# Inverse roots placed one tick later and built from fewer instructions, and the second layer's values copied out of PSUM by VectorE

## The reference, cut to what matters

```python
qkv = h @ wqkv;  q, k, v = jnp.split(qkv, 3, axis=-1)
q = l2norm(q) * qs;  k = l2norm(k) * ksc        # 1 / root of the sum of squares per head
q, k = rotary_xpos(q, k)
o = local_attention(q, k, v)                    # QK_SCALE = 8, window 64, softmax
x = x + o @ wo
h = (h - mu) / jnp.sqrt(var + 1e-05) * lg + lb  # layer norm, then a gated GELU
```

## Time and profile before

| what | us |
|---|---|
| median of 3 runs | 2072.57 (2064.77 to 2075.15) |
| the profiled execution | 2064.33 |
| its span, first to last instruction | 2062.5 |
| TensorE busy | 1760.4 |
| VectorE busy | 1278.5 |
| ScalarE busy | 1186.3 |
| GpSimd busy | 863.4 |

### The profile page before, as it was taken

One profiled execution on the slowest core, in us unless ns is written; L12 is line 12 of the kernel. 1 busy time (PEld: TensorE's weight loads), 2 busy tenths in 40 slices (PEclk: granted clock), 3 DMA queues, 4 the chain that ended last, 5 costly groups with the idle time before them and its releaser, 6 DMA issues.

```text
span 2062.5 us, 38065 instructions
## 1 busy us (share of the span) xinstructions
PE 1760.4 (85%) x12532; PEld 1140.4 (55%) x12532; DVE 1278.5 (62%) x4211; ACT 1186.3 (58%) x3527; POOL 863.4 (42%) x993
## 2 busy tenths in 40 slices
PE   6679988998989888998899888988899797785776
PEld 4358764654566545664566456654566455463454
DVE  4434456566575667566766666666856666857764
ACT  2434547566666666656666675666666565453633
POOL 2633215643445233542544343433453355534640
PEclk9889999999999999999999999999999998897968
DMA  8146510000000000000000000000000000000000
GB/s 235 50 143 224 187 31 1 11 1 1 6 2 17 1 6 1 1 17 1 6 2 17 1 6 2 17 1 5 2 1 11 1 7 1 1 7 0 1 1 11
DMA packets 49724, 53.48 MB, mean 26 GB/s; under 512 B 6386, under 2 KB 42236, under 8 KB 49532
## 3 DMA queue, kind: packets, MB, share of 16 engines
q0 software_dynamic: 7808, 27.79, 4.1%
q1 hardware_dynamic: 41724, 23.26, 3.9%
HBM read 41.60 MB, written 9.44 MB: 25 GB/s over the span
## 4 chain that ended last, share of the span: by engine, by line
PE 47%; DVE 20%; ACT 7%; issue 6%; POOL 1%; DVEq 0%; ACTq 0%; POOLq 0%
PE ps L596 5%; PE ps L658 5%; PE ps L733 3%; PE ps L616 3%; PE ps L575 3%; PE ps L555 3%; DVE p L1042 3%; DVE big L1232 3%; PE ps L640 2%; PE ps L565 2%; DVE ss L1228 2%; PE ps L784 2%; PE ps L630 2%; PE ps L775 2%; PE ps L777 2%
## 5 line engine op out<-in xcount | busy, mean ns | idle before, releaser
L1342 POOL COPY rdx<-rden 128x256 f32<-128x256 f32 x256 | 100.2, 420 | 656.1 <-DVE rden L1059 651.9
L1042 DVE CUSTOM_DVE_ANT_0 p<-ps,mask 128x128 f32<-128x128 f32 (+1 forms) x512 | 152.3, 354 | 209.6 <-PE ps L588 201.8
L1042 DVE CUSTOM_DVE_ANT_0 p<-ps,mask,nrq 128x128 f32<-128x128 f32 x512 | 148.8, 347 | 181.8 <-PE ps L584 181.7
L596 PE MATMUL ps<-ident,p 128*128 128x128 f32 x1280 | 220.9, 297 | 29.2 <-ACT p L873 26.6
L873 ACT ACTIVATE p<-p,nmax 128x128 f32<-128x128 f32 (+1 forms) x512 | 226.3, 442 | 0.0
L872 ACT ACTIVATE p<-p,nmax 128x128 f32<-128x128 f32 x512 | 200.1, 391 | 37.9 <-DVE nmax L1042 37.2
L887 ACT ACTIVATE pt<-ps 128x384 f32<-128x384 f32 (+1 forms) x256 | 111.9, 437 | 190.6 <-PE ps L596 188.6
L733 PE MATMUL ps<-wqkv,hT 128*128 128x512 f32 x384 | 195.2, 617 | 28.5 <-ACT big L952 28.0
L596 PEld LDWEIGHTS ps<-ident,p 128*128 128x128 f32 x1280 | 143.5, 147 | 107.5 <-issue 90.9
L575 PE MATMUL ps<-k,q 64*128 64x128 f32 x1024 | 133.2, 338 | 37.8 <-DVE nmax L1042 17.2
L575 PEld LDWEIGHTS ps<-k,q 64*128 64x128 f32 x1024 | 82.5, 196 | 141.7 <-issue 83.6
(11 more groups left out here) (255 smaller groups left out, 4112.8 us busy)
## 6 DMA issues: line engine op xcount, KB each, us to landing
slots_in<-xn SPq DMA_DIRECT2D x1, 2560.0 KB, 14.3
v<-slots_in SPq DMA_DIRECT2D x20, 128.0 KB, 4.7
slots_out<-v SPq DMA_DIRECT2D x20, 128.0 KB, 1.8
big<-in_x SPq DMA_DIRECT2D x4, 512.0 KB, 6.0
x<-in_x SPq DMA_DIRECT2D x8, 256.0 KB, 3.7
out_x<-x SPq DMA_DIRECT2D x8, 256.0 KB, 2.3
wqkv<-in_wqkv SPq DMA_DIRECT2D x2, 768.0 KB
xn<-in_x SPq DMA_DIRECT2D x6, 256.0 KB, 3.3
```

Of the source, the lines that this page charges most:

```text
L596: last = nc.tensor.transpose(bank[:, j * P:(j + 1) * P], c.p[:, u % 4, j * P:(j + 1) * P], c.ident[:, :])
L1042: last = V.tensor_tensor_reduce(out=c.p[:, u % 4, a:b], in0=bank[:, a:b], in1=mask, scale=scale, scalar=3e38, op0=ALU.add, op1=ALU.min, ac ...
```

## The change

1. `newton_rsqrt` drops the shift (the halving of the bits is one multiplication) and does one cheap step and one longer one in place of three: 9 instructions for 11. The last is returned, not linked, so that the caller can hang its own semaphore on it.
2. `rr` writes the negative root straight to `c.rr`, which now has two halves by turn; `nrq` and the instruction that filled it (L1244) are gone. The factor of 8 went into the rotation table and the mask's constant. `rr` is 10 instructions for 13, `inverse_root` 10 for 12.
3. `rr` of layer 0 moves one tick later for 0 < b < 7, into the tick of `kn` and ahead of it.
4. In layer 1 ScalarE no longer copies v. VectorE does, in a stage `v1` of its own in the tick of that tile's `qkv`, behind the `mix` and `rot` of the tile before. It announces the copy on `v1_done`; TensorE's ring `mm` waits on that semaphore where the bank it wants held such a v. There are 32 such copies of 128x512.

```diff
@@ Plan.qkv_stages
-        self.put(at + TILES, "rr", b, l)
+        for t in range(TILES * l):
+            self.put(at + t, "v1", b, t)
+        self.put(at + TILES + (l == 0 and 0 < b < LAST), "rr", b, l)
         self.put(at + TILES + 1, "kn", b, l)
@@
-def newton_rsqrt(nc, link, r, v, scratch):
+def newton_rsqrt(nc, link, r, v, scratch, t, sign=1):
-    link(nc.vector.tensor_scalar(scratch.bitcast(INT32), v.bitcast(INT32), 1, None, ALU.logical_shift_right))
-    link(nc.vector.tensor_scalar(r.bitcast(INT32), scratch.bitcast(INT32), -1.0, RSQRT_MAGIC, ALU.mult, ALU.add))
-    for _ in range(3):
-        link(nc.vector.scalar_tensor_tensor(out=scratch, in0=r, scalar=-0.5, in1=r, op0=ALU.mult, op1=ALU.mult))
-        link(nc.vector.tensor_tensor(scratch, scratch, v, ALU.mult))
-        link(nc.vector.scalar_tensor_tensor(out=r, in0=scratch, scalar=1.5, in1=r, op0=ALU.add, op1=ALU.mult))
+    a, b, c3 = (sign * x for x in RSQRT_LAST)
+    link(nc.vector.tensor_scalar(r.bitcast(INT32), v.bitcast(INT32), -0.5, RSQRT_MAGIC, ALU.mult, ALU.add))
+    link(nc.vector.tensor_tensor(scratch, r, r, ALU.mult))
+    link(nc.vector.tensor_tensor(scratch, scratch, v, ALU.mult))
+    link(nc.vector.scalar_tensor_tensor(out=r, in0=scratch, scalar=RSQRT_FIRST, in1=r, op0=ALU.add, op1=ALU.mult))
+    link(nc.vector.tensor_tensor(scratch, r, r, ALU.mult))
+    link(nc.vector.tensor_tensor(scratch, scratch, v, ALU.mult))
+    link(nc.vector.tensor_scalar(t, scratch, c3, b, ALU.mult, ALU.add))
+    link(nc.vector.tensor_tensor(t, t, scratch, ALU.mult))
+    return nc.vector.scalar_tensor_tensor(out=r, in0=t, scalar=a, in1=r, op0=ALU.add, op1=ALU.mult)
@@ tensor: mm_bank
-        if mm.free(*name):
-            pe.wait_ge(c.mm_done, mm.free(*name))
+        lane, n = mm.before(*name)
+        if n:
+            pe.wait_ge((c.mm_done, c.v1_done)[lane], n)
@@ scalar: qkv
-        evacuate(c.v1[:, g % 2, t, :], "qkv", b, l, t, 2)
+        if l == 0:
+            evacuate(c.v1[:, g % 2, t, :], "qkv", b, l, t, 2)
@@ vector
+    def v1(b, t):
+        dve.wait_ge(c.mm_full, mm.full("qkv", b, 1, t, 2))
+        V.tensor_copy(c.v1[:, plan.turn[(b, 1)] % 2, t, :], c.mm_ps[mm.slot("qkv", b, 1, t, 2)][:, :]).then_inc(c.v1_done, 1)
+
@@ vector: rr
-        newton_rsqrt(nc, link, c.rr[:, :], c.ss[:, :], c.scratch[:, 0, :])
-        TS(c.nrq[:, g % 2, :, :], c.rr[:, :].rearrange("p (t a h) -> p t a h", t=TILES, a=2)[:, :, 0, :], -8.0, None, ALU.mult)\
+        newton_rsqrt(nc, link, c.rr[:, g % 2, :], c.ss[:, :], c.scratch[:, 0, :], c.scratch[:, 1, :], -1)\
             .then_inc(c.r_ready, 1)
```

More of the change, by code:

```diff
@@ L43 @@
 LAST = BLOCKS - 1
-RSQRT_MAGIC = 1597463007.0
+RSQRT_MAGIC = 1595932665.0
+RSQRT_FIRST = -2.38924456
+RSQRT_LAST = (-1.3199104070663452, 0.4360533356666565, -0.06482572108507156)
 class Common:
@@ L311, in inverse_root @@
     link(nc.vector.tensor_scalar(c.scratch[:, 0, 0:TILES], c.mv[:, :, 1], 1e-5, None, ALU.add))
-    newton_rsqrt(nc, link, c.rstd[:, :], c.scratch[:, 0, 0:TILES], c.scratch[:, 1, 0:TILES])
+    few = c.scratch[:, 1, :]
+    link(newton_rsqrt(nc, link, c.rstd[:, :], c.scratch[:, 0, 0:TILES], few[:, 0:TILES], few[:, TILES:2 * TILES]))
 def whiten(eng, out, x, mv, rstd, t):
@@ L405, in buffers @@
     c.ss = sb("ss", [P, TILES * 2 * HEADS1])
-    c.rr = sb("rr", [P, TILES * 2 * HEADS1])
-    c.nrq = sb("nrq", [P, LAYERS, TILES, HEADS1])
+    c.rr = sb("rr", [P, 2, TILES * 2 * HEADS1])
     c.stats = sb("stats", [P, TILES, 6])
@@ L438, in buffers @@
     c.high_done, c.highs = sem("high_done"), 0
+    c.v1_done = sem("v1_done")
     c.chain, c.pool_chain = sem("chain"), sem("pool_chain")
@@ L490, in count_units @@
                 for j in range(n):
-                    rings[ring].add((*seg, j))
+                    rings[ring].add((*seg, j), lane=int(seg[0] == "qkv" and seg[2] == 1 and j == 2))
             plan.combs[seg] = combs
@@ L603, in values @@
             if st.i == 0:
-                pe.wait_ge(c.mm_done, mm.done("qkv", st.b, st.part, END, 2) if st.kind else mm.done("v", st.b, st.part, END, 0))
+                if st.kind and st.part:
+                    pe.wait_ge(c.v1_done, mm.done("qkv", st.b, 1, END, 2))
+                else:
+                    pe.wait_ge(c.mm_done, mm.done("qkv", st.b, 0, END, 2) if st.kind else mm.done("v", st.b, st.part, END, 0))
         v = c.v1[:, plan.turn[(st.b, st.part)] % 2, :, :] if st.kind else c.v0[:, st.part, :, :]
@@ L1040, in masked @@
                 g = 2 * st.s + i
-                scale = c.nrq[:, turn % 2, g, 2 * st.i + h:2 * st.i + h + 1] if st.kind else -0.125
+                at = g * 2 * HEADS1 + 2 * st.i + h
+                scale = c.rr[:, turn % 2, at:at + 1] if st.kind else -0.125
                 last = V.tensor_tensor_reduce(out=c.p[:, u % 4, a:b], in0=bank[:, a:b], in1=mask,
@@ L1251, in kn @@
         for t in range(TILES):
-            k_over_norm(V, c, t).then_inc(c.kn_ready, 1)
+            k_over_norm(V, c, g % 2, t).then_inc(c.kn_ready, 1)
     def glu(b, l):
@@ L1277, in vector @@
              "ln1n": ln1n, "ln2": ln2, "ln2n": ln2n, "phi": phi, "sum": total, "o1": o1, "s1": s1, "mix": mix, "rot": rot,
-             "rr": rr, "kn": kn, "glu": glu, "down1": down1, "fin": fin}
+             "rr": rr, "kn": kn, "v1": v1, "glu": glu, "down1": down1, "fin": fin}
     for i in range(4):
@@ L1287, in vector @@
     link(last)
-    var, tmp = c.few[:, 0:ALL], c.few[:, ALL:2 * ALL]
+    var, tmp, more = (c.few[:, i * ALL:(i + 1) * ALL] for i in range(3))
     link(TS(var, c.mv_all[:, :, 1], 1e-5, None, ALU.add))
-    newton_rsqrt(nc, link, c.rstd_all[:, :], var, tmp)
+    link(newton_rsqrt(nc, link, c.rstd_all[:, :], var, tmp, more))
     dve.sem_inc(c.stats_ready, 1)
@@ L1322, in vector, with k_over_norm @@
                 stage[seg[0]](*seg[1:])
-def k_over_norm(eng, c, t):
+def k_over_norm(eng, c, turn, t):
     kk = c.qkr[:, t, INNER1:2 * INNER1].rearrange("p (h d) -> p h d", h=HEADS1)
     at = (t * 2 + 1) * HEADS1
-    return eng.tensor_tensor(kk, kk, c.rr[:, at:at + HEADS1].unsqueeze(2).to_broadcast([P, HEADS1, HD]), ALU.mult)
+    return eng.tensor_tensor(kk, kk, c.rr[:, turn, at:at + HEADS1].unsqueeze(2).to_broadcast([P, HEADS1, HD]), ALU.mult)
 def gpsimd(nc, pool, c, plan, mm, s, pt, o, dram):
@@ L1618, in constants @@
     out["c_mask0"] = np.concatenate([np.zeros((P, P), np.float32), causal], 1)
+    far = np.float32(8) * far
     near = np.where((j <= i) & (i <= j + HD), 0, far).astype(np.float32)
@@ L1637, in constants @@
                     np.stack([np.sin(fr) * sc * sign, np.sin(fr) / sc * sign], 1)], 1).astype(np.float32)
+    rot[:, :, 0, :] *= np.float32(-8)
     out["c_rot"] = np.ascontiguousarray(rot.reshape(2, P, 2, 2, HD).transpose(1, 0, 2, 3, 4))
```

## The result

The changed kernel took 2035.69 us (median of 4 runs, 2033.73 to 2037.23) beside 2068.92 of the kernel before: ratio 0.9836, 95% interval 0.9804 to 0.9869, so 1.6% faster. On another chip the same pair gave 2041.86 beside 2069.36, ratio 0.9861 (0.9836 to 0.9886). Predicted were 2051.5, with 2041 as the lower end. The profiled execution took 2037.07 us (its span is 2035.3), 27.3 us less than that of before; the prediction's own sum, in the profiled executions' time, was 20.9.

What follows compares the result with a forecast made beforehand. Bound: TensorE idling where VectorE is late. Terms 10.8 + 3.0 + 1.4 + 5.5 + 0.8 - 0.6 = 20.9 us took the profiled 2064.33 to 2043.4; scaled to the 2072.57 median, 2051.5 was predicted, range 2041 to 2062.

Steps and rivals of the forecast that it cites:

- What bounds the kernel: TensorE is busiest, but its longest waits are for VectorE: keys 39.1 us, h 33.6, s_sb 14.8; VectorE's lateness there counts.
- Every sign that the prediction named for being right: TensorE's waits: s_sb under 3 us, h about 28, keys near 39; VectorE's busy time about even, ScalarE's 19 less.
- The shorter chain ... 16 x 0.39 = 6.3 ... I take 5.5: Layer norms lose two instructions, 0.39 us at each of TensorE's 16 waits for h: 5.5 us gained, bounds 3 and 6.3.
- 0.2 us a block: Layer 0's roots, blocks 2 to 5: allowance for TensorE's clock staying up, raising the gain from 2.5 to 2.7 us.
- The gain is 2.5 us by that sum ... I take 2.7. Four blocks give 10.8: Layer 0's roots one tick later, blocks 2 to 5: wo's copy and logits start 3.1 us earlier; 10.8 us gained.
- Rival (a): Layer 0's gain is given back around kn and down0's copy; only the shorter chain counts: 11.3 us, 2061; chance 0.18.
- its mark of 2 us: Sign of rival (a): TensorE waits 2 us or more for down0's copy (L1095) or nmax in the tick of kn.
- The roots' three instructions, 0.7 us each: rr loses three of 13 instructions, 0.7 us a place; in layer 0's blocks 1 to 6 it is within the tick's sums.
- The values, -0.6: Layer 1's 32 value copies on VectorE: nothing net in blocks 0 to 5, 0.3 us lost in each of the last two.
- the 0.8 worked out: Block 3, layer 1: the product wanting tile 3's bank runs 0.8 us later, ahead of a longer wait for VectorE.
- Rival (c): TensorE short of layer 1's value bank at tiles 1 to 3: 9.3 us a layer, 2126; chance 0.04 with milder forms.
- Rival (b): TensorE's whole idle time and clock come back, 3.9 us in six blocks, 6.3 for norms: 31.3 us, 2041; chance 0.12.

Runs made afterwards that it cites:

- e8_tick_back: The changed kernel with layer 0's roots back in their old tick, short chain kept: 2036.27 us, ratio 0.9853 to the kernel before.

## Why the prediction was wrong

**What bounds the kernel: right, and not enough.** The gain came where TensorE waits for VectorE, and VectorE's busy time hardly moved (1278.5 to 1275.3). Every sign that the prediction named for being right appeared: the waits for `s_sb` (2.0), `h` (27.3) and the keys (37.1), VectorE's busy time, ScalarE's less by 20. They are waits and busy times, and what was missed, TensorE's clock, is in none of them.

**The base took half of the miss.** The prediction was 15.8 us too high. 8.1 of it came from scaling the profiled execution's 2043.4 to the median of the three runs shown. Of that, 3.6 is that 2072.57 was high (with the fourth run the median is 2068.92), and 4.5 that the profiled execution was a fast one of its kernel, while that of the changed kernel was not. 6.3 came from the sum (27.3 for 20.9, rounded), 1.4 from the changed kernel's runs, whose median lies under its profiled one.

**"The shorter chain ... 16 x 0.39 = 6.3 ... I take 5.5": the step that failed.** The length was right (1.58 to 1.19 us of wait). That TensorE's clock behind a norm's wait hangs on that wait was not in the sum. It measured 12.7 in the trace, and 12.1 in the second trace of the same kernel; done alone it measured 20 us in time, and 7.1 in the trace that was kept. I had read that clock behind 3.6 us of idle time, gave it 0.2 us a block, and never looked behind the sixteen waits for `h`, thirteen of which had a slow stretch behind them.

**"The gain is 2.5 us by that sum ... I take 2.7. Four blocks give 10.8": the second.** Each start that I worked out came about, or better: the logits came 3.84 us sooner. What was wrong is that a start won is a gain kept. Shown in block 3: the new 1.50 us wait for `down0`'s copy is followed by 12 us at a granted clock of 0.69 to 0.73, where before it was 1.00. The move is worth nothing alone (1.0002), and in the changed kernel nothing that the times can tell. Rival (a) named the place, `down0`'s copy in the tick of `kn`, and its mark of 2 us was not reached; that nothing but the shorter chain would count was right, and the clock was not in its mechanism. The term of 2.7 us a block measured 1.7, 0.1, 1.3 and 1.6 in blocks 2 to 5, and e8_tick_back has no less in the old tick.

**The roots' three instructions, 0.7 us each: too low.** 22 us alone for 11. By place, in the kernel with the tick back, 7.8 us in the six of layer 0 (4.2 forecast) and 8.3 in five of layer 1 (nothing net forecast). That this surplus is the clock too was not tried apart.

**The values, -0.6: open.** Alone they cost nothing (0.9992), where the same terms without the shorter roots gave 5 to 8 us; in the changed kernel they cost 0 to 13. The wait for the bank came at 11.4 us in eight waits for L746 and L556, 1.1 in block 3 for the 0.8 worked out. Rival (c), with 9.3 us a layer, did not come, although its sign did: new waits for the values' copy were to show it, and small ones appear in the forecast case too.

**Rival (b)**, 31.3 us because idle time and clock come back, was the nearest to the 28 to 34 measured, and had 0.12. It had the size by the wrong places: the clock came back at the norms, where (b) counted only their length.

## What to carry to other kernels

Where TensorE waits a microsecond or two for another engine, look at the granted clock of the few microseconds behind the wait before costing an edit. Here 0.39 us off such a wait was worth 1.9 us in some places, 0.4 in others, and cost 1.2 in two; over the sixteen places it came to between 7 and 18 us for 6.3, by what else the kernel had changed. A wait moved can take the slow stretch with it. Transposes of the identity into the bank that is written next are a cheap trial of that (27 us here with no other change), and with them in place an edit was worth its bare length at the place itself. Gains that come through the clock do not add. One kernel can differ by 0.5% between runs and 0.8% between chips, so what parts are worth has to be compared in the final kernel and on one chip, and one trace of each is too few to say where a surplus of a few microseconds lies.

## What was not expected of the hardware

- 1.58 us without work were followed by 4 us mostly at the lower level, and 1.19 us in the same place were not (0.56 and 1.00). Yet in another place 1.57 us had 1.00 behind them in one trace and 1.16 us had 0.61 in another.
- The same program on the same data ran in 2018 or 2029 us with a mean granted clock of 0.949 or 0.941, and in 2037 on another chip.
- Adding 128 transposes in 16 places made the kernel 19.5 us faster, and the clock stayed up behind all twelve norms of blocks 0 to 5.
